# Layer three's modulation moved from VectorE to ScalarE and GpSimd, with the written order of all three layers re-timed

## The reference, cut to what matters

```
x = x + L0(x)     # three small products with a conditioning vector
x = x + L1(x)     # RMS norm, attention (16 heads of 16), SwiGLU of width 1024
x = x + L2(x)     # attention with a coherence factor per head and token, plus a field term
x = x + L3(x)     # attention with a mask, then norm and modulation
```

```
out  = attention(x) @ Wo.T
rms  = sqrt(mean(out * out) + 1e-6)
xn   = out / rms * rms_scale
shift, sc = split(silu(conditioning) @ Wc.T + bc)
return xn * (1 + sc) + shift
```

## Time and profile before

| | |
|---|---|
| median of three runs | 1535.89 us |
| the profiled execution's own time | 1535.91 us |
| its span, first to last instruction | 1534.1 us |
| PE, matmuls, busy | 1446.8 us (94%) |
| PE, weight loads, busy | 1204.5 us (79%) |
| DVE (VectorE) busy | 1097.2 us (72%) |
| ACT (ScalarE) busy | 705.6 us (46%) |
| POOL (GpSimd) busy | 269.0 us (18%) |

### The profile page before, as it was taken

How to read it: one execution, slowest core, us unless ns; L and a number is a source line. 1 busy time by engine, 2 the same in 40 slices (tenths; PEclk the granted TensorE clock), 3 DMA queues, 4 the chain that set the end, 5 groups by cost and what they waited for, 6 DMA issues and landing times. The chain is left out here.

```text
span 1534.1 us, 29407 instructions
## 1 busy us (share of the span) xinstructions
PE 1446.8 (94%) x10234; PEld 1204.5 (79%) x10282; DVE 1097.2 (72%) x3686; ACT 705.6 (46%) x1539; POOL 269.0 (18%) x323
## 2 busy tenths in 40 slices
PE   2669999999999999999999999999999999999996
PEld 1457888888888888888888787787877887887874
DVE  7757666666666666665656867768678889889884
ACT  1325434343444444433335555555555555555553
POOL 7401000000000000000013232232320111111112
PEclk9879999999999999999999999999999999999998
DMA  7065222332322333232224545445355455445450
GB/s 282 1 86 81 47 40 50 50 50 43 49 42 38 50 50 50 33 63 33 43 43 78 82 57 75 67 61 84 55 75 83 74 77 97 75 76 97 74 77 22
DMA packets 101116, 100.00 MB, mean 65 GB/s; under 512 B 11478, under 2 KB 97624, under 8 KB 100330
## 3 DMA queue, kind: packets, MB, share of 16 engines
q1 hardware_dynamic: 100970, 98.14, 38.1%
HBM read 16.83 MB, written 4.19 MB: 14 GB/s over the span
## 5 line engine op out<-in xcount | busy, mean ns | idle before, releaser
L963 ACT ACTIVATE work<-bank 128x512 f32<-128x512 f32 x768 | 448.6, 598 | 275.9 <-PE bank L1149 223.9
L1149 PE MATMUL bank<-qs,ks 98*128 98x256 f32 x1536 | 410.1, 350 | 0.5 <-DMA qs<-nm 0.5
L528 DVE TENSOR_REDUCE rowmax<-bank 128x2 f32<-128x512 f32 x512 | 337.7, 679 | 100.6 <-PE bank L1139 99.9
L1139 PE MATMUL bank<-ks,qs 96*128 96x256 f32 x1536 | 337.6, 302 | 21.4 <-DMA ks<-qk_lo 10.0
L1149 PEld LDWEIGHTS bank<-qs,ks 98*128 98x128 f32 x1536 | 277.3, 192 | 37.3 <-issue 6.0
L1139 PEld LDWEIGHTS bank<-ks,qs 96*128 96x128 f32 x1536 | 243.2, 191 | 45.1 <-DMA ks<-qk_lo 16.9
L525 DVE CUSTOM_DVE_ANT_0 c1t<-bank,big_q 128x256 bf16<-128x256 f32 x512 | 190.3, 420 | 0.4
L1161 PE MATMUL bank<-work,vp 128*32 128x256 f32 x3072 | 185.7, 382 | 0.0
L989 ACT ACTIVATE work<-bank 128x256 f32<-128x256 f32 x128 | 49.0, 383 | 235.3 <-PE bank L1198 235.3
L583 DVE SCALAR_TENSOR_TENSOR work<-work,bank 128x256 f32<-128x256 f32 x128 | 53.4, 418 | 128.8 <-ACT work L989 127.7
L1161 PEld LDWEIGHTS bank<-work,vp 128*32 128x32 f32 x3072 | 90.0, 109 | 62.4 <-ACT work L963 0.2
(11 more groups left out here) (209 smaller groups left out, 1813.5 us busy)
## 6 DMA issues: line engine op xcount, KB each, us to landing
qs<-qk_hi SPq DMA_DIRECT2D x192, 128.0 KB, 3.9
ks<-qk_hi SPq DMA_DIRECT2D x192, 128.0 KB, 3.8
qs<-qk_lo SPq DMA_DIRECT2D x96, 128.0 KB, 4.4
ks<-qk_lo SPq DMA_DIRECT2D x96, 128.0 KB, 4.3
xres<-in_x_t SPq DMA_DIRECT2D x4, 1024.0 KB, 9.0
x_in<-in_x SPq DMA_DIRECT2D x16, 256.0 KB, 2.8
out<-xres SPq DMA_DIRECT2D x16, 256.0 KB, 2.1
qs<-nm SPq DMA_DIRECT2D x96, 16.0 KB
```

Source lines behind the costliest of these rows:

```text
L528: a = dve.tensor_reduce(rowmax[:, :, k:k + 1], bank[:, :].rearrange("p (t s) -> p t s", t=TC), AX, ALU.max)
L963: act.activation(probs[:, place[n, b, k], :, :], bank[:, :].rearrange("p (c s) -> p c s", c=TC), ACT.Exp, scale=HD ** -0.5)\
L1139: m = pe.matmul(bank[:, t * S:(t + 1) * S], qs[par][0:SCORE_ROWS, k, t * P:(t + 1) * P], ks[par][0:SCORE_ROWS, k, :], start=True, stop=True)
L1149: m = pe.matmul(bank[:, c * S:(c + 1) * S], ks[par][0:SHIFTED_ROWS, k, c * P:(c + 1) * P], qs[par][0:SHIFTED_ROWS, k, :], start=(n != 3), ...
```

## The change

Layer three's VectorE work of `mod` and `resid` is taken away. ScalarE copies the modulation rows (`act.copy`), and scales `acc_bank` by the inverse root only (two `activation` with `ACT.Copy`, 128x256). GpSimd gets one more instruction of 128x512 ahead of its two: the multiplication by `mod_a`. `mod_sum` counts four per batch instead of three. The time table `SLOT` of all three layers is changed too, and one number of `LATER`.

```diff
-        "max": (-6.11, 4.35), ... "stack": (-25.3, -22.08, -15.9, -16.88), ... "ffn": (25.73, 1.15)
+        "max": (-6.29, 4.35), ... "stack": (-25.3, -22.08, -15.97, -16.88), ... "ffn": (25.73, 1.11)
...
     2: {
-        "neg": (-6.46, 1.15), ... "k": -24.09, ... "coh3": -10.31, ... "sumv": 4.0
+        "neg": (-7.45, 1.15), ... "k": -22.73, ... "coh3": -10.48, ... "sumv": 5.23
     3: {
-        "norm": (10.2, 15.99), "neg": (-6.23, 1.31), "q": -24.57, "stack": (-24.46, -20.12, -15.9, -15.03), "v": -13.4, "squares": 23.07
+        "norm": (12.06, 15.93), "neg": (-6.53, 2.22), "q": -24.17, "stack": (-24.46, -19.29, -15.9, -15.03), "v": -12.83, "squares": 22.54
...
-LATER = {"vector": {... "xn": 0.23 ...}}
+LATER = {"vector": {... "xn": 0.11 ...}}
...
-        mod_ok, mod_sum, stored = ev("mod_ok", 1), ev("mod_sum", 3), ev("stored", 16)
+        mod_ok, mod_sum, stored = ev("mod_ok", 1), ev("mod_sum", 4), ev("stored", 16)
... (VectorE: the branches "mod" and "resid" are gone)
... (GpSimd, "resid")
                         pool.wait_ge(mod_sum.sem, mod_sum.at(b, 2))
+                        pool.wait_ge(mod_ok.sem, mod_ok.at(b, 1))
+                        pool.tensor_tensor(y[:], y[:], mod_a[:, :].rearrange("p (a d) -> p a d", a=1).to_broadcast([P, TC, D]), ALU.mult)\
+                            .then_inc(mod_sum.sem, 1)
+                        pool.wait_ge(mod_sum.sem, mod_sum.at(b, 3))
                         pool.tensor_tensor(y[:], y[:], mod_s[:, :].rearrange("p (a d) -> p a d", a=1).to_broadcast([P, TC, D]), ALU.add)\
                             .then_inc(mod_sum.sem, 1)
-                        pool.wait_ge(mod_sum.sem, mod_sum.at(b, 3))
+                        pool.wait_ge(mod_sum.sem, mod_sum.at(b, 4))
                         pool.tensor_tensor(xres[:, b, :, :], xres[:, b, :, :], y[:], ALU.add).then_inc(L.x_new.sem, 1)
... (ScalarE)
+                    if what == "mod":
+                        if b:
+                            act.wait_ge(L.x_new.sem, L.x_new.at(b, 0))
+                        else:
+                            act.wait_ge(on_field.sem, on_field.at(NBATCH, 0))
+                        act.wait_ge(mod_full.sem, mod_full.at(b, 1))
+                        act.copy(x_in[:], acc_bank[:, :].rearrange("p (a d) -> p a d", a=2)).then_inc(mod_ok.sem, 1)
+                    if what == "resid":
+                        act.wait_ge(inv3.sem, inv3.at(b, 1))
+                        if b:
+                            act.wait_ge(L.x_new.sem, L.x_new.at(b, 0))
+                        else:
+                            act.wait_ge(lay[2].x_new.sem, lay[2].x_new.at(NBATCH, 0))
+                        for t in range(TC):
+                            act.activation(y[:, t, :], acc_bank[:, t * D:(t + 1) * D], ACT.Copy, scale=statb[:, 2, t:t + 1]).then_inc(mod_sum.sem, 1)
```

More of the change, by code:

```diff
@@ L42 @@
         "smax": -13.9, "pv": (8.3, 16.3), "rz": (8.59, 16.41), "norm": (8.44, 16.81), "neg": (-6.41, 1.59),
-        "max": (-6.11, 4.35), "xT": -26.99, "q": -24.35, "stack": (-25.3, -22.08, -15.9, -16.88), "k": -22.83, "v": -12.2,
+        "max": (-6.29, 4.35), "xT": -26.99, "q": -24.35, "stack": (-25.3, -22.08, -15.97, -16.88), "k": -22.83, "v": -12.2,
         "load": -46, "rank": -32.95, "cond": -30.74, "squares": -30.51, "xn": -28.27, "oT": 18.5, "wo": 21.54, "yn": 23.31,
-        "yT": 24.38, "ffn": (25.73, 1.15), "down": (27.4, 1.24)},
+        "yT": 24.38, "ffn": (25.73, 1.11), "down": (27.4, 1.24)},
@@ L46 @@
     2: {
-        "smax": -14.72, "pv": (9.43, 17.26), "rz": (9.93, 17.56), "norm": (14.07, 17.86), "neg": (-6.46, 1.15),
-        "max": (-6.52, 2.71), "xT": -26.47, "q": -24.49, "stack": (-23.72, -22.05, -15.9, -15.63), "k": -24.09, "v": -11.32,
-        "load": -30, "coh1": -13.18, "coh2": -10.81, "coh3": -10.31, "vsum": 1.0, "sumv": 4.0, "field": 5.0, "oT": 19.5,
+        "smax": -14.72, "pv": (9.43, 17.26), "rz": (9.93, 17.56), "norm": (14.07, 17.86), "neg": (-7.45, 1.15),
+        "max": (-6.52, 2.71), "xT": -26.47, "q": -24.49, "stack": (-23.72, -22.05, -15.9, -15.63), "k": -22.73, "v": -11.32,
@@ L50 @@
+        "load": -30, "coh1": -13.18, "coh2": -10.81, "coh3": -10.48, "vsum": 1.0, "sumv": 5.23, "field": 5.0, "oT": 19.5,
         "wo": 22.05},
     3: {
-        "smax": -13.86, "pv": (9.2, 15.39), "rz": (9.7, 15.69), "norm": (10.2, 15.99), "neg": (-6.23, 1.31),
-        "max": (-6.13, 2.38), "xT": -26.55, "q": -24.57, "stack": (-24.46, -20.12, -15.9, -15.03), "k": -21.53, "v": -13.4,
-        "mod": 14.15, "oT": 16.94, "wo": 20.71, "squares": 23.07, "resid": 24.6},
+        "smax": -13.86, "pv": (9.2, 15.39), "rz": (9.7, 15.69), "norm": (12.06, 15.93), "neg": (-6.53, 2.22),
@@ L55 @@
+        "max": (-6.13, 2.38), "xT": -26.55, "q": -24.17, "stack": (-24.46, -19.29, -15.9, -15.03), "k": -21.53, "v": -12.83,
+        "mod": 14.15, "oT": 16.94, "wo": 20.71, "squares": 22.54, "resid": 24.6},
 }
-LATER = {"vector": {"q": -0.2, "k": 0.5, "ffn": 0.3, "oT": 0.5, "field": -0.34, "pv": 0.6, "coh2": 0.46, "squares": 0.41, "rz": 0.8, "norm": 1.2, "v": -0.29, "xn": 0.23, "stack": 1.16, "xT": -0.21}, "scalar": {"wo": 1.0, "pv": 0.2, "yn": -0.02, "oT": -0.25, "xn": -0.04, "ffn": -0.24, "xT": -0.33}, "gpsimd": {"max": -0.28, "oT": -0.14, "q": -0.42, "xn": -0.41}, "sync": {"k": -0.01}}
+LATER = {"vector": {"q": -0.2, "k": 0.5, "ffn": 0.3, "oT": 0.5, "field": -0.34, "pv": 0.6, "coh2": 0.46, "squares": 0.41, "rz": 0.8, "norm": 1.2, "v": -0.29, "xn": 0.11, "stack": 1.16, "xT": -0.21}, "scalar": {"wo": 1.0, "pv": 0.2, "yn": -0.02, "oT": -0.25, "xn": -0.04, "ffn": -0.24, "xT": -0.33}, "gpsimd": {"max": -0.28, "oT": -0.14, "q": -0.42, "xn": -0.41}, "sync": {"k": -0.01}}
@@ L593, in step @@
                             .then_inc(L.x_new.sem, 1)
[L594 to L609, removed]
                 return step
```

## The result

| | before | after |
|---|---|---|
| median of six runs, us | 1536.65 (1534.87 to 1538.51) | 1529.51 (1525.19 to 1530.24) |
| profiled execution / span, us | 1535.91 / 1534.1 | 1529.24 / 1527.5 |

The ratio is 0.9949, 95% interval [0.9937, 0.9961]. The sign was right and the size was not: 1520.5 was forecast, 1514 to 1529 the range. The two spans differ by 6.6 us where the sum said 15.4.

A forecast was written before the change was run, and what follows sets the result against it. TensorE's matmuls were taken to be busy nearly throughout, with time to give back mainly in layer two; from 1535.91 us, -6.4 - 4.2 - 2.0 - 2.8 = -15.4 gave 1520.5 us, range 1514 to 1529 (the forecast's own 1515 to 1526).

The forecast's parts named there:

- Layer two, row maxima and stack of k: Layer two: shorter waits for row maxima save 6.4 us, and the wait for k's stack transfer goes, saving 4.2.
- The signs that were named: Layer two: low-part-of-k wait row gone, row-maxima row smaller, no VectorE idle before `smax` 7, batch 0.7 to 0.8 us shorter.
- the one that multiplied a steady batch by fourteen: Layer two: 0.46 us a batch from the row maxima, taken for 14 batches, 6.4 us.
- A new row of `probs` waiting for k: Sign of being wrong: a new row of L1147, L1149 or L1161 waiting for ScalarE or for k.
- Layer three, TensorE's gap: Layer three, steady: the wait of `smax` 11 for k's bank shrinks by 0.14 us a batch, 2.0 in all.
- The stack of k has about 0.7: Layer three, SyncE: GpSimd's third instruction delays store and transfers by 0.2 to 0.4 us; k's stack has room of about 0.7.
- Rival (b): Layer three gives nothing or loses, as L536 is held by a whole GpSimd instruction (1.27): 1526.8 us, chance 0.15.
- The end: Last batches: shorter waits and a clock staying up, less added costs, sum to -2.8 us, bounds -4.6 and +1.2.
- the copy's price of 0: Layer three: ScalarE's copy before `probs` 15 delays the last exponential 0.25 us, covered before `pv` 3; value 0.
- rival (c): ScalarE late before `pv` 3: the copy holds `probs` 15, TensorE stands 0.9 us in 15 batches; 1540.0 us, chance 0.05.
- The third GpSimd instruction: The end: one more GpSimd instruction after the last `wo` costs 1.26 us, less 0.1 for ScalarE against VectorE.
- Layer one: Layer one: TensorE has no wait to lose and the moved steps fit; value 0, bounds 0 and +4.5 us.

The follow-up runs named there:

- k_all: The changed kernel with k of layer two put back to its old place in all batches; 1531.75 us, ratio 0.9972.
- k_switch: The changed kernel with k of layer two's batches 0 to 2 at its old place; 1528.16 us, ratio 0.9942.
- three_repairs: The changed kernel with store_behind's edit, batches 14 and 15 modulated as before, and k of layer two's batches 0 to 3 in its old place; 1518.76 us.
- slots_only: The kernel before with only the changed kernel's table `SLOT`; VectorE still copies and modulates; 1524.54 us, ratio 0.9921.
- store_behind: The changed kernel with layer three's output transfer issued behind k's stack on SyncE; 1525.4 us, ratio 0.9924.
- copy_back: The changed kernel with the last batch's copy of the modulation row back on VectorE; 1526.5 us, ratio 0.9936.
- three_repairs_again: three_repairs unchanged, measured again on the same chip; 1519.41 us, ratio 0.9886 against the kernel before.

## Why the prediction was right in layer two and wrong in the sum

- **Layer two, row maxima and stack of k** (-6.4 and -4.2): right, place by place and in size. -10.1 over thirteen batches, and k_all splits it in 0.43 and 0.30 a batch where 0.46 and 0.30 were worked out. The signs that were named came: the row for the low part of k is gone, that for the maxima is smaller, and VectorE has no idle before `smax` 7.
- **The switch** (no term at all): +4.0. This is the largest error, 4.0 of 8.8 us. The step that failed is the one that multiplied a steady batch by fourteen and took the first batches for free. k was moved past a wait that exists only in the last batch of layer one, which it had been filling. Only the first two batches of layer two are concerned, and no group of rows looked there. Of the 4.0, about 1.5 are the longer wait in batch 0, 1.7 the clock behind it, and 0.7 stand in batch 1, which has the second wait. k_switch shows the mechanism for the first wait, three_repairs (k of batch 3 too) for the second. A new row of `probs` waiting for k was one of the signs of being wrong that the prediction named.
- **Layer three, TensorE's gap** (-0.14 a batch): the mechanism was right and the size small, 0.26. Places alone give 0.11 (slots_only 22.88), the moved work 0.15.
- **"The stack of k has about 0.7"** (price 0): this step failed. The room was there before, 5.4 us less landings of 3.9 to 4.5, so 0.9 at least, and the third GpSimd instruction took about the 0.2 to 0.4 that were given for it. Left out were the gain of 0.26 a batch, by which `smax` 0 wants the stack sooner, and landings that grew to 5.1 to 5.6 in six batches. These lost 4.0 us in sum, which store_behind gives back (299.5 to 295.5); the stretch is 2.4 us off the forecast, since the gain was larger than foreseen. Why the landings grew in some batches and not in others stays open.
- **Rival (b), L536 held for a whole instruction**: no. L534 took 0.47 and L536 0.17 in a steady batch:

```profile
1304.63 1.28 POOL L751 TENSOR_TENSOR y<-y,x_in 128x512 f32<-128x512 f32 x1 [1.83 <-ACT y L981]
...
1305.47 0.47 DVE L534 TENSOR_SCALAR negs<-rowmax 128x16 fp32r<-128x16 f32 x1
1305.97 0.17 DVE L536 SCALAR_TENSOR_TENSOR negs<-rowmax,negs 128x16 fp32r<-128x16 f32 x1
...
1305.99 1.30 POOL L754 TENSOR_TENSOR y<-y,x_in 128x512 f32<-128x512 f32 x1
```

  L534 ends when L751 does, and L536 starts 0.02 us ahead of L754: it slips between two GpSimd instructions that follow one another, as the prediction took it. L536 took at most 0.18 us in all of its 96 times. By the Trainium skill (SBUF — State Buffer, Who interferes with whom) the one that starts first keeps the ports that the two share for its whole instruction, and the other is blocked. The trace agrees: L534 started under L751 and was held, L536 started ahead of L754 and was not, so the rule did not ask for rival (b) here.
- **The end** (-2.8): the gains of batch 14 were all there, 1.5 + 1.2 + 1.7. The step that failed is the copy's price of 0. Batch 15 cost what rival (c) describes, ScalarE late before `pv` 3 because the copy holds the exponential, which had been priced at 15 batches or none; but what the copy waits for is GpSimd's last instruction of batch 14 and not the `mod` matmul. It happens in one batch, and there it costs 1.4 and, with the clock, 3.1 (copy_back). The copy was checked in a steady batch only. The third GpSimd instruction was priced right: 1.26 less 0.1 against 1.2 measured.
- **Layer one** (0): right in the steady part (41.58 and 41.57 us a batch). The 1.2 us less up to its end lie within what traces of one and the same order differ by there (2.9).

## What to carry to other kernels

A gain worked out in the steady batch holds for the steady batches; walk every moved step through the first and the last batch of each stage as well, where the steps around it are others and where a filler may be the only thing over a long wait. When work goes to an engine whose queue is in order, ask for each new instruction what it waits for in the last, shortest batch. A transfer's margin is its window less its landing; the window shrinks with every gain elsewhere in the batch, and the landing is no constant (3.6 to 5.6 us here for one and the same transfer). Read it for the transfer that is waited for, and take the longest.

## What the hardware did that was not expected

- A short pause can cost more than its length, and where the clock falls is not given by one pause. In the changed kernel a pause of 2.27 us was followed by 3.4 us at half clock at once; in slots_only the wait for `yn` is 2.3 us too, and the clock stayed at 1.00 from 775 to 779 and fell at 828 (granted 0.66 from 827 to 832). The last `wo` stood behind a pause of 2.15 us in every trace. In the five where `pv` 3 had waited 1.06 us or more some 3 us before, it took 3.07 to 3.75 us; in six of the seven others it took 1.97, and in the seventh, three_repairs_again, 2.92. So the earlier pause goes with the fall but is not needed for it. No run here says more of what decides it. That the changed kernel's runs spread from 1525.2 to 1530.2 may come from this; it was not shown.
- One and the same transfer of 128 KB, the low part of k for the first eight heads in layer three, landed 3.9 to 4.5 us after its issue before the change, 3.9 to 5.6 after it and 3.6 to 4.0 in store_behind. All the stack transfers of layer three lie between 3.1 and 6.0 us in these three traces.
- `yn` (L578, 128x256, SBUF to SBUF) takes 1.35 us in the median and 0.34 at best: at the switch the two of a batch take 2.62 us beside GpSimd's L742 and L765, and each starts when one of these is already running. The Trainium skill (SBUF — State Buffer, Who interferes with whom) counts `tensor_scalar`, which `yn` is, among the VectorE instructions that can contend with GpSimd for the shared ports, and the trace agrees. This is what makes the wait that k had filled so long. GpSimd's two, between 771.98 and 774.52 (`yn` from 772.05 to 774.67):

```profile
771.98 1.27 POOL L742 TENSOR_TENSOR xres<-xres,y 128x512 f32<-128x512 f32 x1
773.21 1.31 POOL L765 TENSOR_TENSOR xres<-xres,bout_rows 128x512 f32<-128x512 f32 x1
```
